# Second cross-attention: the expert additions spread over VectorE's step, the transposed rows copied by ScalarE

## The reference

```python
x = x + _L0_ffn_ref(_layernorm(x, axis=-1), ...)          # routed experts + shared expert
x = x + _L1_xattn_ref(_layernorm(x, axis=-1), ctx_1024, ctx_1024)

def _L1_xattn_ref(qm, km, vm):
    scale = 1.0 / jnp.sqrt(jnp.asarray(qm.shape[-1], dtype=qm.dtype))
    qkm = jnp.einsum('bqd,bkd->bqk', qm, km) * scale
    out = jnp.einsum('bqk,bkd->bqd', qkm, vm)
    return jax.nn.softmax(out, axis=-1)
```

## Time and profile before

| | us |
|---|---|
| median of 3 runs | 2430.57 |
| lowest and highest | 2427.62, 2439.83 |
| profiled execution, its own time | 2439.46 |
| its span, first to last instruction | 2437.7 |
| second cross-attention in it: first transfer issued to last update's end | 1604.62 to 1785.49 |
| its 24 steps in the loop | 1639.57 to 1766.94, 127.37 |
| VectorE busy over the span | 1493.9 (61%) |
| TensorE busy over the span | 2143.7 (88%) |

### The profile page before, as it was taken

How to read it: one execution, slowest core, us unless ns; L and a number is a source line. 1 busy time by engine, 2 the same in 40 slices (tenths; PEclk the granted TensorE clock), 3 DMA queues, 4 the chain that set the end, 5 groups by cost and what they waited for, 6 DMA issues and landing times. The chain is left out here.

```text
span 2437.7 us, 57593 instructions
## 1 busy us (share of the span) xinstructions
PE 2143.7 (88%) x19514; PEld 1597.1 (66%) x19527; DVE 1493.9 (61%) x4179; ACT 1098.7 (45%) x2377; POOL 981.1 (40%) x1105
## 2 busy tenths in 40 slices
PE   4999999999879998998999999969968888477773
PEld 3888888888779986565666666646658877233332
DVE  3777777777556654882333333347757776587772
ACT  2666666666534442283222222223335554335442
POOL 3444445444300003343666666611133343035455
PEclk9999999999878978999999999989989999789996
DMA  4110111100011003041222222245510000000002
GB/s 131 32 30 29 29 29 30 38 29 29 8 20 11 9 10 106 0 190 33 85 85 84 87 86 86 82 167 205 191 25 8 9 8 8 35 1 1 0 0 69
DMA packets 120654, 128.80 MB, mean 53 GB/s; under 512 B 77681, under 2 KB 95218, under 8 KB 119282
## 3 DMA queue, kind: packets, MB, share of 16 engines
q1 hardware_dynamic: 106306, 89.77, 12.1%
q0 software_dynamic: 13824, 37.77, 5.0%
q10 hardware_dynamic: 432, 0.07, 0.0%
HBM read 96.11 MB, written 27.26 MB: 51 GB/s over the span
## 5 line engine op out<-in xcount | busy, mean ns | idle before, releaser
L426 ACT ACTIVATE xa_prob<-xa_neg_s,xa_neg_max 128x256 f32<-128x256 f32 x512 | 224.5, 499 | 142.5 <-DVE xa_neg_max L314 142.5
L1847 PE MATMUL ex_ps_h<-moew_w,ex_xT 128*128 x576 | 275.1, 600 | 4.1 <-issue 2.3
L314 DVE CUSTOM_DVE_ANT_0 xa_neg_s<-xa_ps_s,xa_mask 128x256 f32<-128x256 f32 x512 | 191.4, 421 | 37.6 <-PE xa_ps_s L480 22.0
L1895 DVE COPY ex_xT<-ex_ps_x 128x256 f32<-128x256 f32 x144 | 61.1, 425 | 247.9 <-PE ex_ps_x L1854 116.7
L1824 POOL DMA_INDIRECT ex_xg<-xn_rows,moe_in_row x144 | 139.6, 970 | 110.3 <-issue 63.2
L509 PEld LDWEIGHTS xa_ps_o<-xa_v,xa_probT 128*64 128x64 f32 x4096 | 141.3, 138 | 48.3 <-issue 43.0
L433 ACT ACTIVATE xa_probT<-xa_ps_s 128x512 f32<-128x512 f32 x256 | 152.0, 594 | 42.1 <-PE xa_ps_s L491 39.6
L509 PE MATMUL xa_ps_o<-xa_v,xa_probT 128*64 128x34 f32 x4096 | 170.2, 228 | 0.0
L1829 POOL DMA_INDIRECT expert_outs<-ex_y,moe_out_row x144 | 142.1, 987 | 62.0 <-issue 35.9
L491 PE MATMUL xa_ps_s<-g_ident,xa_prob 128*128 128x128 f32 x1024 | 164.1, 283 | 2.9 <-ACT xa_prob L426 2.4
L1880 ACT ACTIVATE ex_act_g<-ex_ps_h 128x256 f32<-128x256 f32 x144 | 55.2, 383 | 244.7 <-PE ex_ps_h L1847 144.7
(11 more groups left out here) (314 smaller groups left out, 5027.8 us busy)
## 6 DMA issues: line engine op xcount, KB each, us to landing
xa_ctxT<-in_ctxT_dram SPq DMA_DIRECT2D x32, 512.0 KB, 3.6
xb_ctx_rows<-in_ctx_rows_dram SPq DMA_DIRECT2D x32, 512.0 KB, 3.7
xb_expert_y<-expert_outs SPq DMA_DIRECT2D x32, 512.0 KB, 4.5
moew_w<-in_moe_w_dram SPq DMA_DIRECT2D x8, 1024.0 KB, 13.2
g_x<-in_x_dram SPq DMA_DIRECT2D x4, 1024.0 KB, 9.6
sa_v<-sa_vs SPq DMA_DIRECT2D x128, 32.0 KB, 2.2
xn_rows<-rs_xn SPq DMA_DIRECT2D x8, 512.0 KB, 2.9
moew_xw<-in_moe_w_dram SPq DMA_DIRECT2D x8, 512.0 KB, 20.7
```

Source lines behind the costliest of these rows:

```text
L314: ins = nc.vector.tensor_tensor_reduce(neg_s[:, u % 2, g, :], ps_s[j][:, g * S:(g + 1) * S], mask[:, b, :], -1.0, 3e38, ALU.add, ALU.min, ...
L426: ins = nc.scalar.activation(prob[:, u % 2, i, :], neg_s[:, u % 2, i, :], ACT.Exp, bias=neg_max[:, u % 2, i:i + 1], scale=-1.0)
L1847: mm = nc.tensor.matmul(ps_h[1 - par][:, :], xT[:, 1 - par, k, :], c.w1[:, own, k, :], start=(k == 0), stop=(k == KC - 1))
```

## The change

On ScalarE, the copy of the transposed rows `ps_x` to `xT` is added at the head of the step, ahead of exp. On VectorE that copy is gone, the first addition stands ahead of the row maximum, the reciprocal stands ahead of the fourth, and the update of `X` by the softmax now stands ahead of mean and variance.

```diff
@@ ScalarE
             def step(s, q):
                 m, o = s - 3, s - 5
                 par = 1 - q % 2
+                if live(m):
+                    act.wait_ge(xT_done, m + 1)
+                    wait(act, o_done, m - 1)
+                    nc.scalar.activation(xT[:, par, :, :], ps_x[par][:, 0:E].rearrange("p (k t) -> p k t", k=KC),
+                                         ACT.Copy).then_inc(xT_ready, 1)
                 if live(o):
                     act.wait_ge(max_ready, o + 1)
@@ VectorE
+                def add(k):
+                    wait(dve, added, TOP * l + k)
+                    nc.vector.scalar_tensor_tensor(X[:, l, :], expert_y[:, (q - 2) % 4, k, :],
+                                                   c.weight[:, l, k:k + 1], X[:, l, :],
+                                                   ALU.mult, ALU.add).then_inc(added, 1)
                 if live(t):
                     ln.normalise(dve, nc, t, 1 - par, xT_done)
+                if live(l):
+                    dve.wait_ge(gathered[(q - 2) % 4], (l - (q - 2) % 4) * 4 + 16)
+                    add(0)
                 if live(o):
                     dve.wait_ge(o_done, o + 1)
                     nc.vector.tensor_reduce(neg_max[:, 1 - par:2 - par], ps_o[1 - par][:, 0:E], AX.X, ALU.max,
                                             negate=True).then_inc(max_ready, 1)
                 if live(l):
-                    dve.wait_ge(gathered[(q - 2) % 4], (l - (q - 2) % 4) * 4 + 16)
-                    for k in range(TOP):
-                        wait(dve, added, TOP * l + k)
...
-                if live(t):
-                    dve.wait_ge(xT_done, t + 1)
-                    wait(dve, o_done, t - 1)
-                    nc.vector.tensor_copy(xT[:, 1 - par, :, :], ps_x[1 - par][:, 0:E].rearrange("p (k t) -> p k t", k=KC))\
-                        .then_inc(xT_ready, 1)
+                    add(1)
+                    add(2)
+                if live(o):
+                    dve.wait_ge(exp_ready, o + 1)
+                    nc.vector.reciprocal(rz[:, 1 - par:2 - par], total[:, 1 - par:2 - par]).then_inc(rz_ready, 1)
+                if live(l):
+                    add(3)
+                if live(o):
+                    dve.wait_ge(rz_ready, o + 1)
+                    nc.vector.scalar_tensor_tensor(X[:, o, :], ex[:, 1 - par, :], rz[:, 1 - par:2 - par], X[:, o, :],
+                                                   ALU.mult, ALU.add).then_inc(x_updated, 1)
                 if live(l):
                     wait_apart(dve, added, TOP * l + TOP, c.passed_dve)
                     ln.statistics(dve, nc, l, par)
-                if live(o):
-                    dve.wait_ge(exp_ready, o + 1)
...
```

More of the change, by code:

```diff
@@ L2019, in step @@
                 if live(l):
-                    dve.wait_ge(gathered[(q - 2) % 4], (l - (q - 2) % 4) * 4 + 16)
-                    for k in range(TOP):
-                        wait(dve, added, TOP * l + k)
-                        nc.vector.scalar_tensor_tensor(X[:, l, :], expert_y[:, (q - 2) % 4, k, :],
-                                                       c.weight[:, l, k:k + 1], X[:, l, :],
-                                                       ALU.mult, ALU.add).then_inc(added, 1)
-                if live(t):
-                    dve.wait_ge(xT_done, t + 1)
-                    wait(dve, o_done, t - 1)
-                    nc.vector.tensor_copy(xT[:, 1 - par, :, :], ps_x[1 - par][:, 0:E].rearrange("p (k t) -> p k t", k=KC))\
-                        .then_inc(xT_ready, 1)
+                    add(1)
[9 more added lines that the diff above has]
+                                                   ALU.mult, ALU.add).then_inc(x_updated, 1)
                 if live(l):
```

## The result

| | us |
|---|---|
| changed kernel, median of 17 runs | 2423.82 (2417.43 to 2427.65) |
| kernel before, median of 17 runs | 2431.59 (2425.37 to 2439.83) |
| ratio | 0.9968, 95% interval 0.9957 to 0.9979 |
| profiled execution after, span | 2421.4 |
| loop of the second cross-attention, after | 119.79 (before 127.37) |

The change gains 7.8 us by the medians, 0.3%, inside what was forecast (2424.1, range 2416 to 2432) and inside the 0.5% that counted as no change. Timed once more, beside other kernels, it stood at 2419.44 against 2423.69, a ratio of 0.9978 (0.9968 to 0.9987). Both intervals exclude no gain; together they reach from 0.1 to 0.4%.

The account below looks back on a forecast made before the run. The prediction took the loop to be bound by a circle between VectorE and GpSimd. Loop -7.2, written-out steps -0.2 and exp's table load +0.9 gave -6.5 us, from 2430.57 to 2424.1 us, range 2416 to 2432.

Parts of the forecast that it names:

- the circle of VectorE and GpSimd: In the loop, VectorE's start-to-start distances plus GpSimd's answer set the step: 5.31 us before, 5.01 expected with the turn's end.
- The turn's end: In the loop, the end of each four-step turn adds 0.20 us to its fourth step, 0.05 a step when spread.
- The choice between bounds: On VectorE, third to fourth addition, around the reciprocal: between 0.617 and 0.71 us, 0.62 taken.
- GpSimd's clean shadow: In the loop, L137 to the next normalising without VectorE's update beside it: 1.28 instead of 1.51 us, mean -0.15 a step.
- ScalarE's slack: In the loop, exp's sum seen at 1.93 us, asked for at 2.08: slack 0.15, so the new copy is barely hidden.
- The load of exp's table: Once on ScalarE, the 1.28 us load now stands behind the copy and delays the next normalising: +0.9 us, bounds 0 and 1.3.
- Written-out steps: Five steps outside the loop, bound by TensorE at 4.85 us, at best 4.79: -0.3 us at most, -0.2 taken.
- A: Rival on VectorE: additions cost 0.617 us before whatever follows, so spreading saves nothing; +0.09 a step, 2433.5 us; chance 0.1.
- B: Rival: ScalarE becomes late, by a 0.60 us copy or later exp sum; +0.15 a step, 2427.7 us; chance 0.22.
- C: Rival: TensorE's floor is reached, the loop step falls to 4.85 us, the time to 2420.3; chance 0.15.
- D: Rival: a real loss, such as exp so late that the reciprocal holds VectorE 0.8 us a step; 12 us; chance 0.03.

Follow-up runs that it names:

- e2: Changed kernel's order on VectorE, but VectorE keeps the copy, between second and third addition, and ScalarE has none; loop 122.21 us against the changed kernel's 119.79.
- e3: Changed kernel with the four additions together again behind the maximum, then reciprocal and update; loop 131.22 us against the changed kernel's 119.79.
- e7: Changed kernel's spread additions, but the copy stays on VectorE and stands with the update behind the statistics, copy first; loop 118.68 us, median 2422.11.
- e4: Changed kernel with one move, the update of X behind the statistics again; loop 118.14 us against the changed kernel's 119.79.
- e5: Changed kernel with ScalarE's copy behind exp instead of ahead of it; loop 119.78 us against the changed kernel's 119.79.
- e6: Changed kernel with a second, unused copy of the transposed rows on ScalarE ahead of the first; loop 120.48 us against the changed kernel's 119.79.
- e1: Kernel before with one edit: ScalarE copies the transposed rows ahead of exp, VectorE's order otherwise as it was; loop 125.94 us against 127.37 before.
- e11: Changed kernel with the update behind the statistics, ScalarE's copy behind exp, and all steps written out; 24 steps 116.26 us, median 2413.86.

## Why the prediction was right

*The bound.* Right as named: the circle of VectorE and GpSimd, not VectorE's work. e2, e3 and e7 show it from three sides.

*What was luck.* That the median came within 0.3 us of 2424.1. The gain was 1.3 us larger than forecast, and the kernel before was 1.0 us slower in its 17 runs than in the 3 that the forecast started from. The range from 2416 to 2432 also contained no change at all (2430.57), so the times alone bear out little; the terms below do.

*The terms.* Predicted and measured: first addition to maximum 0.40, 0.39; maximum to second 0.33, 0.34; second to third 0.617, 0.62; third to fourth 0.62, 0.61; fourth to update 0.40, 0.40; update to statistics 0.40, 0.40; L137 to normalising 1.28, 1.27. The circle 4.96, 4.93 or 4.94. The turn's end came out as 0.21 in one step of four, 0.20 assumed. Loop: -7.2 predicted, -7.58 measured.

*The choice between bounds.* For third to fourth addition I took 0.62 out of 0.617 to 0.71, because the follower does not need the reciprocal's result. The 0.61 bears that out; the upper bound would have made the loop 2.2 us longer.

*GpSimd's clean shadow.* L141 is 0.22 in all steps. What I had not seen is what lies behind its 0.45: in the steps in which the update started first, the end of L141 is tied to the update's end, and its length follows from that. I had the same fact as two kinds of steps and priced it right here, but the wrong reading made e4's expectation 3 us too high.

*ScalarE's slack.* The step was right, the number was not. I gave 0.15, counted from 1.93, when VectorE sees exp's sum; the sum itself was to be out at 1.89, 0.19 ahead of the reciprocal. In the step shown above it is out 1.81 behind the normalising and asked for at 2.07: 0.26, to be held against the 0.19. The mis-sized term is copy to exp: I used the copy's length, 0.38, and exp follows the copy by 0.30 there and by 0.28 in the third and fourth steps of a turn. (The 0.30 is not the copy's: with the copy behind exp, in e5, exp starts 1.25 behind the normalising in that step as well, held by the maximum.) Start-to-start distances, which I used on VectorE, were needed on ScalarE too. e6 confirms the 0.26 by using it up. In the first step of a turn the slack is 0.16, which I had not looked at separately.

*The load of exp's table.* Predicted +0.9, bounds 0 to 1.3. Measured 5.71 against 4.87 between the transposes of steps 5 and 6, +0.84; e5 takes it back, and e1 shows that it also needs the reciprocal on the circle.

*Written-out steps.* I had given them -0.2. The changed kernel shows 4.85 and 4.84, so there is next to nothing. The transposes of steps 7 and 8, at the loop's start, were 5.17 apart before and are 4.84 now; that I had not counted.

*The sum.* -6.5 forecast; by the medians -7.8 and, in the second comparison, -4.3. The stage in the profiles is 8.0 shorter, but its first TensorE step ran partly at half clock (granted 0.50 up to 1619.6 before, 1606.7 after, 1609.6 in the second profile of the changed kernel), and there the profiles differ although the kernels do the same: transposes of steps 3 and 4 are 6.53 apart before, 5.48 after and 6.55 in the second profile of the changed kernel. In that second one the stage takes 1768.00 - 1594.76 = 173.24, 7.6 less than before. The half clock is thus worth a microsecond either way. From the transposes of step 4 (1620.44, 1608.60 and 1610.35), behind the half clock in all three, to the end of the last update the stage takes 165.05 before, 157.79 after and 157.65 in the second profile: 7.3 and 7.4 us less, which is the figure to hold against the forecast's 6.5.

*The rivals.* A (spacing is no wait) falls by the row itself, 0.39 and 0.34 around the maximum, and by e3. With it falls, for these shapes, what was cited beside it of waits: a semaphore wait of one VectorE instruction on the one before has a price here, 0.62 against 0.40. An instruction that waits for nothing even starts before the record of the one ahead has ended: 0.33 behind a maximum of 0.42, 0.40 behind an addition of 0.48. B did not come, because of the larger slack. C was the nearest miss: in the changed kernel TensorE still waits 0.31 for the normalising in a turn's first step, and in the others its transposes come 4.89 to 4.94 apart; e11 is that case, with 4.84 a step. D had no ground.

## What to carry to other kernels

Add up the start-to-start distances around the circle that closes a step, not the busy time and not the idle time: VectorE's idle time before the normalising rose from 15.6 to 27.5 us while the loop got shorter by 7.6. Chains of dependent instructions on one engine should be filled with independent ones of the same step, where each can cost a fraction of its distance (0.11 of 0.33 in e2); and an instruction moved out of such a gap leaves the wait behind, which is why the copy alone brought 1.4 us and not 7.9. Where a step in a hardware loop is slower than the same step written out, look first for register instructions behind a wait: here they and the turn's end were worth 10.6 us in 24 steps, more than the reordering, and with them gone the reordering was worth 0.5.

## What the runs showed of the hardware

- From one addition to an independent instruction VectorE takes 0.40 us. To an addition that waits for the one before it takes 0.52 where the step is written out and 0.617 in the loop, where a register instruction for the address stands behind the wait: the wait costs 0.12 and 0.22.
- GpSimd's `L141`, when VectorE's two-input update started ahead of it, ended 0.08 us after the update ended, at different offsets (lengths 0.45, 0.35 and 0.25); started ahead of the update, it took 0.22.
- ScalarE follows a 0.38 us copy from PSUM after 0.27 to 0.28 us, where nothing else holds the next instruction.
- The load of the exp table (1.28 us) costs nothing where ScalarE idles. Behind a copy that waits for TensorE it cost 0.84 to 0.86 us once where the next normalising needed exp's result, and nothing in e1, where it did not.
- 37 steps written out, where the loop kernel holds 17 (an estimate of some 1000 TensorE instructions more, from 26 products and their weight loads a step), showed no cost of their own in the trace: TensorE was busy 116.77 of 116.77 us.
